# A graph network on one core: part of a gather moved into an earlier stage, index columns kept on chip, loops with branch hints

## The reference

```
source_x = take(node_x, sources); target_x = take(node_x, targets)
message_x = mlp(concat(source_x, target_x, edge_x))      # relu between two products
agg = segment_sum(message_x, targets)
out = mlp(concat(agg, node_x))
```

## Time and profile before

| | us |
|---|---|
| median of 3 runs | 11421.91 (11396.03 to 11455.06) |
| the profiled execution | 11435.44 |
| its span | 11433.6 |
| TensorE busy | 8072.5 (71%) |
| VectorE busy | 6568.7 (57%) |
| ScalarE busy | 3727.7 (33%) |
| GpSimd busy | 3197.6 (28%) |

### The profile page before, as it was taken

One profiled execution on the slowest core, in us unless ns is written; L12 is line 12 of the kernel. 1 busy time (PEld: TensorE's weight loads), 2 busy tenths in 40 slices (PEclk: granted clock), 3 DMA queues, 4 the chain that ended last, 5 costly groups with the idle time before them and its releaser, 6 DMA issues. The chain is left out here.

```text
span 11433.6 us, 265027 instructions
## 1 busy us (share of the span) xinstructions
PE 8072.5 (71%) x91323; PEld 7370.6 (64%) x91323; DVE 6568.7 (57%) x19944; ACT 3727.7 (33%) x6597; POOL 3197.6 (28%) x3201
## 2 busy tenths in 40 slices
PE   5475555555555778888887899899955666666666
PEld 5343444444444668888786899899954566565565
DVE  3796222222222379989998799699943444444444
ACT  1000111111111245555554577467721111111111
POOL 0102555555555000000000000000015555555552
PEclk9866666666666589999999799799956666666666
DMA  3201111111111032222222233133311111111111
GB/s 52 18 11 21 39 42 40 40 41 40 41 41 42 19 97 83 82 83 82 83 82 66 66 99 98 46 100 99 98 26 21 20 20 21 20 21 21 20 20 21
DMA packets 702357, 566.54 MB, mean 50 GB/s; under 512 B 453974, under 2 KB 557494, under 8 KB 701496
## 3 DMA queue, kind: packets, MB, share of 16 engines
q1 hardware_dynamic: 601272, 452.33, 15.3%
q0 software_dynamic: 100352, 104.57, 5.5%
HBM read 529.75 MB, written 26.76 MB: 49 GB/s over the span
## 5 line engine op out<-in xcount | busy, mean ns | idle before, releaser
L754 POOL DMA_INDIRECT msg_G<-msg_src,msg_idx x1568 | 1537.7, 981 | 1829.4 <-DMA msg_dcol<-dst_kept 1368.2
L754 POOL DMA_INDIRECT soft_G<-soft,soft_idx x1568 | 1573.4, 1003 | 1229.0 <-issue 640.9
L1634 ACT ACTIVATE sage_G<-ps 128x384 bf16<-128x384 f32 (+1 forms) x2650 | 1284.7, 485 | 499.9 <-PE ps L1645 493.3
L633 POOL MEMSET acc<- 96x1280 f32 x30 | 34.4, 1163 | 4693.9 <-POOLq L1247 2538.9
L1645 PE MATMUL ps<-T,sage_ohT 128*128 128x192 bf16 x10388 | 1305.4, 247 | 17.3 <-DVE sage_ohT L1602 17.3
L1657 PE MATMUL ps<-sage_G,sage_ohd 128*128 128x192 bf16 x10388 | 1287.3, 245 | 0.0
L1608 DVE TENSOR_SCALAR sage_ohd<-iota,sage_cols 128x256 bf16<-128x256 bf16 x5194 | 1138.6, 280 | 92.6 <-PE ps L1657 65.7
L1490 PE MATMUL ps<-att_far,att_ohT 128*128 128x65 bf16 x15582 | 949.4, 197 | 269.7 <-DVE att_ohT L1441 219.7
L1490 PE MATMUL ps<-acc,att_ohT 128*128 128x65 bf16 x15582 | 945.6, 197 | 2.1 <-issue 1.9
L923 PE MATMUL ps<-msg_winp,msg_OHT 128*128 128x64 bf16 x4704 | 417.4, 207 | 740.5 <-issue 737.8
L1645 PEld LDWEIGHTS ps<-T,sage_ohT 128*128 128x128 bf16 x10388 | 905.1, 98 | 27.7 <-DVE sage_ohT L1602 17.7
(11 more groups left out here) (436 smaller groups left out, 16110.1 us busy)
## 6 DMA issues: line engine op xcount, KB each, us to landing
sage_rows<-srow SPq DMA_DIRECT2D x424, 320.0 KB, 3.4
acc<-pair_rows SPq DMA_DIRECT2D x196, 448.0 KB, 3.8
att_rows<-pair_rows SPq DMA_DIRECT2D x147, 448.0 KB, 3.8
msg_edge<-edge_attr SPq DMA_DIRECT2D x196, 256.0 KB
sage_rows<-srow SPq DMA_DIRECT2D x106, 288.0 KB, 3.4
msg_G<-msg_src,msg_idx POOLq DMA_INDIRECT x1568
soft_G<-soft,soft_idx POOLq DMA_INDIRECT x1568
att_rows<-pair_rows SPq DMA_DIRECT2D x49, 256.0 KB, 3.5
```

The costliest lines, as they stand in the source:

```text
L633: done(pool.memset(acc[0:TOP, nodes], 0.0), "zeroed")
L754: eng.indirect_dma_start(B["G"][h][:, j, :], None, src_table, bass.IndirectOffsetOnAxis(ap=B["idx"][h][:, j:j + 1], axis=0)).then_inc(gath ...
L1634: act.activation(G[s % RING][:, 0:m, :], ps[:, s % RING, 0:m * 3 * D].rearrange("p (c n) -> p c n", c=m), ACT.Copy).then_inc(S["taken"], 1)
```

## The change

- `gather_kept(pool)`, in slot building's GpSimd part behind the two iotas: for the 49 chunks c < 195 with c mod 8 in KEPT = (2, 6), eight indirect DMAs each from `msg_src` by the columns of `srci`, into a ring of KRING = 4 parts of `acc`; two chunks later each is stored by a GpSimd DMA to `kept_rows` in DRAM (256 KB). At the end it waits for the stores and clears that part of `acc`, which `zero_sums` now leaves out.
- In the msg pass those chunks aren't gathered; SP loads them from `kept_rows` into `G` (`load_kept`, lag 0). The window and edge loads come at lag 2 instead of 4.
- `src` is loaded with `dst` at the start, ahead of it in the same list, and both stay in SBUF (`srci`, `dstf`) until after the msg pass; they are loaded again in a block by themselves before *after_sage2*, for the soft pass. The two column loads per chunk and their waits are gone in both passes. ScalarE copies the chunk's indices into `idx` (`copy_indices`, lag 0, first in its list), and a gather waits for that copy.
- Every inner loop is made by `loop()`, which sets `hint_back_edge=True`: one hint instruction at the head of a turn.

```diff
+KEPT = (2, 6)
+KRING = 4
+    def loop(eng, start, end):
+        return nc.Fori(start, end, engines=bass.OrderedEngineSet([eng.engine]), hint_back_edge=True)
...
+        kept_chunks = [c for c in range(C - 1) if c % U in KEPT]
+        kept_rows = dram("kept_rows", (len(kept_chunks), P, TPC * D))
...
+        srci = edge_cols.enter_context(nc.sbuf_tensor("srci", [P, C, TPC], I32))
...
-            for t, v in ((dsti, a["dst"]),):
+            for t, v in ((srci, a["src"]), (dsti, a["dst"])):
...
-                        with eng.Fori(1, C // U) as i:
+                        with loop(eng, 1, C // U) as i:
...
                     def gather(eng, c, h, turn):
+                        if h in kept:
+                            return
                         eng.wait_ge(S[rows_user], at(c, U))
-                        wait_columns(eng, h, turn)
+                        eng.wait_ge(S["idx"], at(c))
...
-                            chunks(sp, (0, load_columns), (LEAD, load_rows))
+                                def load_kept(c, h, turn, last):
+                                    if h in kept:
+                                        sp.wait_ge(S[rows_user], at(c, U))
+                                        hold(sp)
+                                        q = (turn + -1) * len(kept) + kept.index(h)
+                                        sp.dma_start(B["G"][h][:].rearrange("p j d -> p (j d)"), kept_rows[bass.ds(q, 1)].rearrange("o p n -> p (o n)")).then_inc(kept_in[h], 16)
+
+                                chunks(sp, (0, load_kept), (2, body))
...
-            K["wait_columns"](dve, h, turn)
-            dve.wait_ge(S["oh"], at(c, 2))
-            dve.tensor_scalar(B["drel"][b][:], B["dcol"][h][:], base_bc[:, bass.ds(c, 1)], None, ALU.subtract).then_inc(S["drel"], 1)
+            dve.tensor_scalar(B["drel"][b][:], cols_of(dstf, c), base_bc[:, bass.ds(c, 1)], None, ALU.subtract).then_inc(S["drel"], 1)
...
+        def copy_indices(K, act, c, h, turn):
+            S, B, at = K["S"], K["B"], K["at"]
+            act.wait_ge(S[K["rows_user"]], at(c, U))
+            hold(act)
+            act.activation(B["idx"][h][:], cols_of(srci, c), ACT.Copy).then_inc(S["idx"], 1)
...
+        def gather_kept(pool):
+
+            def store(q):
+                pool.wait_ge(gathered[q % KRING], (q // KRING + 1) * (16 * TPC))
+                pool.dma_start(kept_rows[q], kept_G[q % KRING].rearrange("p j d -> p (j d)")).then_inc(stored[q % KRING], 16)
+
+            for q, c in enumerate(kept_chunks):
+                if q >= KRING:
+                    pool.wait_ge(stored[q % KRING], (q // KRING) * 16)
+                for j in range(TPC):
+                    pool.indirect_dma_start(kept_G[q % KRING][:, j, :], None, msg_src, bass.IndirectOffsetOnAxis(
+                        ap=srci[:, c, j:j + 1], axis=0)).then_inc(gathered[q % KRING], 16)
+                if q >= 2:
+                    store(q - 2)
...
+            gather_kept(pool)
...
+        with nc.Block() as block:
+            @block.sync
+            def _(sp):
+                sp.dma_start(dstf[:].rearrange("p c j -> p (c j)"), dst_kept[:]).then_inc(again, 16)
+                sp.dma_start(srci[:, 0:C - 1, :], by_edge(a["src"], 0, C - 1)).then_inc(again, 16)
+                sp.dma_start(srci[:, C - 1:C, :], by_edge(a["src"], E - CE, 1)).then_inc(again, 16)
+                sp.wait_ge(again, 48)
```

More of the change, by code:

```diff
@@ L649, in gnn_kernel @@
         gathered = [sem(f"gathered{k}") for k in range(U)]
+        stored = [sem(f"kept_stored{k}") for k in range(KRING)]
         s_const, n_const = sem("constant_columns"), [0]
@@ L757, in edge_pass @@
                     with nc.Block() as block:
[L758 to L773, removed]
-                                    hold(sp)
-                                    with nc.allow_non_contiguous_dma("a window's column"):
-                                        sp.dma_start(B["win"][b][:], win_table[bass.ds(first, P), 0:wcols]).then_inc(loaded[b], 16)
-                                if edges:
-                                    sp.wait_ge(S["edge_turned"], at(c, 2))
-                                    hold(sp)
-                                    lo = E - CE if last else c * CE
-                                    rows = a["edge_attr_64"][bass.ds(lo, CE), :].rearrange("(p j) d -> p j d", j=TPC)
-                                    sp.dma_start(B["edge"][b][:], rows).then_inc(loaded[b], 16)
-                            chunks(sp, (0, load_columns), (LEAD, load_rows))
@@ L808, in _ @@
                         def _(eng):
[L809 removed]
+                            landed = [(k not in kept) * (C // U + (k < C % U)) * (16 * TPC) for k in range(U)]
                             for s, n in zip(gathered, landed):
[L811 removed]
+                                if n:
+                                    eng.wait_ge(s, n)
                             eng.inc_swdge_sem(gathered, landed, mode="sub")
@@ L1080, in every @@
                     if not isinstance(groups, int):
-                        with eng.Fori(0, groups) as i:
+                        with loop(eng, 0, groups) as i:
                             for lag, f in sorted(stages, key=lambda stage: stage[0]):
@@ L1093, in every @@
                         step(0, k, depth)
-                    with eng.Fori(1, groups // depth) as i:
+                    with loop(eng, 1, groups // depth) as i:
                         for k in range(depth):
@@ L1309, in run_steps @@
                 step(0, k, n)
-            with eng.Fori(1, iterations) as i:
+            with loop(eng, 1, iterations) as i:
                 for k in range(n):
@@ L1954, in gnn_kernel @@
               [(soft, "hN", D + 2, "row", 3), (soft_dst, "tS", 1, "row", 3)])
-        edge_pass("soft", "drel oh oh_turned oht mrow old top new u l em ratio spread rows e1 e2 e3 e4 ex msg scaled top_row sums acc",
+        edge_pass("soft", "drel oh idx oh_turned oht mrow old top new u l em ratio spread rows e1 e2 e3 e4 ex msg scaled top_row sums acc",
                   soft, D + 2,
```

64 lines of the change are left out of this document (47 added, 17 removed).

## The result

The changed kernel takes 10,978.53 us in the median of four runs (10,943.23 to 11,012.01), beside 11,408.97 us of the kernel before on the same chip: a ratio of 0.9622, 95% interval 0.9593 to 0.9651. It is 3.8% faster, 430 us. The forecast was 11,411 us, no change.

A forecast was written before the change was run, and what follows sets the result against it. No engine was taken to be the bound for long; gather streams slow TensorE. Terms 500 - 440 - 75 - 30 + 15 + 19 = -11 give 11,424 us against the profiled 11,435.4, 11,411 by the median; range 10,900 to 11,700.

The forecast's parts named there:

- the likeliest case: Whole kernel: all terms as summed, 11,411 us, own range 11,270 to 11,550; chance 0.62.
- rival B: Slot building is untouched by the gathers, as TensorE's slow rate needs something of the msg pass; 10,911 us, chance 0.13.
- Slot building, +500: Gathers moved into slot building hold TensorE to 0.4 matmuls a us, so the stage ends 500 us later.
- The msg pass, -440: Fewer gathers in the msg pass cut a turn of eight chunks from 110.5 to 92.5 us, 440 us less.
- second of its two models: Msg pass loop: each stretch of gathers keeps its free start, loss 29 us, a turn 90 us, 500 us less.
- Hints, -75: Attention loop: branch hints cut TensorE's 90.4 us of "issue" waits at the loop's start, 75 us less.
- -30 in the soft pass: Soft edge pass: hints save a third of VectorE's 103.5 us of like waits, 30 us less.
- Reloads, +34: The src loads at the start cost 15 us, the second reload before the last SAGE phase 19 us.
- The soft pass, 0 and -30: Soft edge pass: 30 us less from hints, otherwise no change, as all 196 chunks are gathered as before.
- D: Both edge passes: the index copy lets gathers go a chunk too late, +137 msg, +173 soft; 11,751 us, chance 0.15.

The follow-up runs named there:

- a_kept3: The changed kernel with three chunks in eight kept (73 chunks) instead of two (49); 10,838 us, ratio 0.9604 to the kernel before.
- a_pace3: The changed kernel with a 128x256 memset on GpSimd behind each gather of the edge passes, without a drain; 10,382 us, ratio 0.9187 to the kernel before.
- a_nohints: The changed kernel without the branch hints; 9,507 us, ratio 0.9556 to the kernel before.
- a_nokept: The changed kernel with no kept chunks, all 196 gathered in the msg pass; 9,912 us, ratio 0.9969 to the kernel before.
- a_lags2: The changed kernel with ScalarE's own steps one chunk later in both edge passes; 10,952 us, ratio 0.9693 to the kernel before.

## Why the prediction was right and wrong

The time lay in the range of 10,900 to 11,700, but the likeliest case, no change at 11,411, failed: the kernel gained 430 us. The time lies 67 us above the centre of rival B, to which I gave 0.13, and that nearness is partly luck: beside B's sum the msg pass gained 117 us more and the soft pass lost 172 more.

- **Slot building, +500: wrong, +37.** The step that failed is the choice of the row: "I take 500, because the unbroken stream at 1080 is the nearest row." It took the cause to be that the stream has no break. In slot building it has none either, 392 gathers in 642 us; but they are 1.64 us apart in the mean and not 1.25, since VectorE works beside them on two SBUF inputs: in `a_kept3` the same gathers shrink from 1,246 to 947 ns when it falls idle. `a_pace3` shows by one edit that distance decides whether TensorE is held back in the msg pass, where the earlier trace rows were read. That it also decides in slot building is argued from this and not shown: no run had gathers 1.25 us apart beside slot building's own work. I had read the distance off a stage in which VectorE is nearly idle, and carried it to one where it is 98% busy. The rate of 0.4 matmuls a us was one draw as well: another held trace of the same kernel has 110 matmuls in those 73 us and not 29.
- **Rival B had the time; its reason is open.** It said that the slow rate needs something of the pass beside the gathers. The pass's loads and float32 matmuls don't suffice: in `a_pace3` they are there and the slow rate isn't. That they are needed too isn't ruled out, since dense gathers ran beside no work of TensorE but that of the two edge passes. But B has slot building untouched, and on held chips it isn't quite (14 to 37 us). The Trainium skill's rule ("SBUF — State Buffer", "Who interferes with whom") that PE never waits on anyone gave B's time; it does not describe the held batches (29 to 110 matmuls in 73 us), and in the free ones the rows agree with it (437).
- **The msg pass, -440: right in its mechanism, -557.** "A turn 90" was the second of its two models (the loss falls from 49 to 29 us because each stretch keeps its free start); measured 88.1, with a loss of 29.6. I took 92.5, between the models, which gave away some 60 us. The turn also came out 2 us below the second model, some 50 us in all: TensorE's own work was 58.5 us a turn and not 61.3, at a granted clock of 0.73 in the loop and not 0.69. In a free batch the pass gains 463 us (1,980 to 1,517), by the plain count of 10 us of gathering per kept chunk; that the two kinds of chip gain about as much, for different reasons, is chance.
- **Hints, -75: right, -57**, and 52 between `a_nohints` and the kernels with hints. Of the -30 in the soft pass 16 to 24 are there in a free batch; in a held one they can't be told apart. That VectorE's loop there gains from the hint, which the prediction said no row showed, the trace does show: 114 packets of instructions before, one after, and VectorE's wait of the earlier trace rows falls from 103.5 to 55.1 us (104.2 and 26.1 in the free batches). In the attention loop the packets only fall from 504 (4090 to 6230) to 365 (3600 to 5650): there the hint takes away the wait, and not the fetching.
- **Reloads, +34: measured +25.** The src loads cost 14.2 us of issue, and the first phase starts at 61.07, as forecast; by the first iota 6 of these 15 us are made up, where wasn't looked into.
- **The soft pass, 0 and -30: wrong, +142 to the last gather and -18 behind it.** In all held runs with the changed columns and no filler it is 2,785 to 2,878 us against 2,676 and 2,736; in free ones 2,026 to 2,050. So on held chips it lost 49 us or more; on a free one nothing of the kind shows, as the change of columns costs some 23 us there in all (`a_nokept`), which is the reloads. D named the late release of the gathers; `a_lags2` moves that release and the pass stays long. Nor are GpSimd's waits shorter, in which TensorE could catch up: 587.8 us in 74 waits for the columns before, 921.6 in 118 for the index copy after, 7.9 and 7.8 us each. There are more of them. Why stays open.
- **What I left out altogether** is that TensorE's being held back isn't the kernel's alone: 1,340 to 1,470 us of the time of the kernel before are there on one chip and not on another. With the profile of one execution that can't be seen. For a free chip the sum would have been another one; with the terms as they were measured later it is 9,957 - 490 for gathers - 54 for hints + 25 for reloads = 9,438, beside a measured 9,457.

## What to carry to other kernels

A slow rate seen beside a transfer has a density as well as a presence: before carrying its price to another stage, work out the distance of the transfers there, with what the neighbours do to it. Work that is moved under a stage bound by VectorE may be slowed by it, and here that is probably what made it nearly free. And where an engine waits on "issue" beside a dense stream of another, spacing the stream is worth one run, though it must be measured on more than one chip.

## What the runs showed of the hardware

- In some batches streams of indirect DMAs on GpSimd 1.25 us apart (128 rows of 256 bytes each) hold TensorE's instructions back in the two edge passes, without any wait that the profile shows and without fetches of instructions: 29 to 110 matmuls in 73 us against 437 on another chip. It begins 11 us into a stream. At 1.28 us apart inside a chunk (1.40 in the mean) it is weaker; at 1.44 (1.59) it is all but gone in the msg pass (0.8 us a turn at the product, 12.1 without a filler).
- An indirect DMA of this kind costs GpSimd 0.95 us and 0.30 of issue. A 128x64 memset behind it (0.17 us) adds only 0.03 to the distance inside a chunk, a 128x256 one (0.33 us) 0.19. A drain and the larger memset behind each gather make it 3.4 us. Beside a VectorE that is 96% busy on slot building (574 of 600 us) the same DMA takes 1,246 ns in the mean, beside an idle one 947 (`a_kept3`).
- A hint at the loop's head takes a back edge of TensorE from about 4 us to 0.5 or less, in a loop where it had such a wait at all.
